# The remainders of the message tiles in a GNN edge loop: from GpSimd and VectorE to VectorE alone

## The reference, cut to what matters

```python
src, dst = edge_index
edge_feat = concatenate([x[src], x[dst], edge_attr], axis=-1)     # 512 + 512 + 64
h = mish(edge_feat @ W1 + b1)
messages = mish(h @ W2 + b2)                                      # 20000 x 512
agg = segment_sum(messages, dst, num_segments=1250)
```

## Time and profile before

| what | value |
|---|---|
| median of 3 runs | 1195.03 us (1194.22 to 1196.01) |
| the profiled execution | 1194.06 us, span of its instructions 1192.5 us |
| granted TensorE clock, mean of the span | 0.932 of full speed |
| PE busy / DVE / ACT / POOL, share of the span | 89% / 81% / 70% / 58% |

### The profile page before, as it was taken

How to read it: one execution, slowest core, us unless ns; L and a number is a source line. 1 busy time by engine, 2 the same in 40 slices (tenths; PEclk the granted TensorE clock), 3 DMA queues, 4 the chain that set the end, 5 groups by cost and what they waited for, 6 DMA issues and landing times. The chain is left out here.

```text
span 1192.5 us, 19301 instructions
## 1 busy us (share of the span) xinstructions
PE 1063.1 (89%) x5651; PEld 883.6 (74%) x5651; DVE 966.3 (81%) x1640; ACT 839.1 (70%) x1025; POOL 691.2 (58%) x541
## 2 busy tenths in 40 slices
PE   3993999999999999999999999998499995659974
PEld 2772888888888888888888888886277774559962
DVE  6651699999999999999999999999648775733366
ACT  3212899999999999999999999998235451434442
POOL 3245777777787777778778777861312210554310
PEclk9996999999999999999999999999699995779975
DMA  6736766666666666666666666660201111735545
GB/s 176 254 119 148 152 129 136 131 131 137 130 133 133 129 135 131 133 136 133 129 129 136 132 131 130 132 137 34 71 1 44 35 52 58 219 114 152 149 125 176
DMA packets 129771, 148.82 MB, mean 125 GB/s; under 512 B 73254, under 2 KB 81863, under 8 KB 129598
## 3 DMA queue, kind: packets, MB, share of 16 engines
q0 software_dynamic: 39280, 97.61, 38.3%
q1 hardware_dynamic: 90381, 50.03, 16.0%
q10 hardware_dynamic: 16, 0.02, 0.0%
HBM read 137.02 MB, written 15.69 MB: 128 GB/s over the span
## 5 line engine op out<-in xcount | busy, mean ns | idle before, releaser
L938 PE MATMUL ps<-W2h,w1l_w3l 128*128 128x512 f32 x1264 | 426.1, 398 | 0.0
L788 POOL DMA_INDIRECT gath<-dst_table,idx_sl x158 | 263.9, 1670 | 54.0 <-issue 47.1
L938 PEld LDWEIGHTS ps<-W2h,w1l_w3l 128*128 128x128 f32 x1264 | 227.4, 189 | 38.1
L938 PE MATMUL ps<-W2l,w1l_w3l 128*128 128x512 f32 x632 | 247.7, 392 | 0.0
L801 POOL DMA_INDIRECT gath<-src_table,idx_sl x156 | 188.7, 1210 | 98.5 <-issue 52.9
L810 POOL TENSOR_TENSOR msg_lo<-act,msg_hi 128x512 fp32r<-128x512 f32 x79 | 126.4, 1600 | 35.4 <-DVE msg_hi L922 35.4
L938 PEld LDWEIGHTS ps<-W2l,w1l_w3l 128*128 128x128 f32 x632 | 119.0, 188 | 26.5
L872 DVE TENSOR_TENSOR agg<-agg,ps 125x512 f32 x166 | 114.2, 688 | 15.3 <-PE ps L982 10.8
L827 ACT ACTIVATE act<-ps 128x1024 f32<-128x1024 f32 x79 | 81.2, 1027 | 37.4 <-PE ps L970 37.0
L902 DVE SCALAR_TENSOR_TENSOR act<-act,ps 128x1024 f32<-128x1024 f32 x79 | 96.0, 1215 | 2.5 <-ACT act L855 2.5
L884 DVE SCALAR_TENSOR_TENSOR act<-act,ps 128x1024 f32<-128x1024 f32 x79 | 96.0, 1215 | 2.1 <-ACT act L846 2.1
(11 more groups left out here) (321 smaller groups left out, 2380.3 us busy)
## 6 DMA issues: line engine op xcount, KB each, us to landing
f_w_raw<-in_L_ffn_w_dram SPq DMA_DIRECT2D x32, 512.0 KB, 4.6
ea_sl<-ea_scr SPq DMA_DIRECT2D x158, 64.0 KB
ea_scr<-in_edge_attr_dram POOLq DMA_DIRECT2D x1, 5000.0 KB, 19.0
w_raw<-in_L_gnn_W_dram SPq DMA_DIRECT2D x3, 1024.0 KB, 10.8
gath<-src_table,idx_sl POOLq DMA_INDIRECT x158, 3.7
gath<-dst_table,idx_sl POOLq DMA_INDIRECT x158
x_raw<-in_x_dram SPq DMA_DIRECT2D x5, 448.0 KB
src_table<-tabs SPq DMA_DIRECT2D x10, 224.0 KB
```

Source lines behind the costliest of these rows:

```text
L788: pool.indirect_dma_start(out=gath[:, k, j, :], out_offset=None, in_=dst_table[:, :], in_offset=bass.IndirectOffsetOnAxis(ap=idx_sl[:, p % ...
L938: return nc.tensor.matmul(ps_2[:, p % 2, j, :], part[:, p % 2, d, j * P:(j + 1) * P], weights[:, d, :], start=False, stop=last)
```

## The change

VectorE's subtraction L894 covers both tiles of the pair instead of the first, GpSimd's subtraction L810 is gone, and the two semaphores of the halves become one, on which ScalarE (for the free slot of `act2`) and TensorE (before L982) wait.

```diff
 # GpSimd, in step s
                 if p > 0 and exists(p):
                     add_destinations(p)
-                p = s - 4
-                if exists(p):
-                    pool.wait_ge(S["msg_hi_ready"], p + 1)
-                    need(pool, S["sum_ps"], ring_free(p))
-                    nc.gpsimd.tensor_tensor(msg_lo[:, ring(p)][:, 1], act2[:, p % A2, 1], f32(msg_hi[:, ring(p)][:, 1]), ALU.subtract).then_inc(S["msg_lo1_ready"], 1)
 # ScalarE, ahead of L833
-                        act.wait_ge(S["msg_lo0_ready"], g - A2 + 1)
-                        act.wait_ge(S["msg_lo1_ready"], g - A2 + 1)
+                        act.wait_ge(S["msg_lo_ready"], g - A2 + 1)
 # VectorE, L894
-                    nc.vector.tensor_tensor(msg_lo[:, ring(m)][:, 0], a4[:, 0], f32(msg_hi[:, ring(m)][:, 0]), ALU.subtract).then_inc(S["msg_lo0_ready"], 1)
+                    nc.vector.tensor_tensor(msg_lo[:, ring(m)], a4, f32(msg_hi[:, ring(m)]), ALU.subtract).then_inc(S["msg_lo_ready"], 1)
 # TensorE, ahead of L982
-                    pe.wait_ge(S["msg_lo0_ready"], min(m + 1, PAIRS))
-                    pe.wait_ge(S["msg_lo1_ready"], min(m + 1, PAIRS))
+                    pe.wait_ge(S["msg_lo_ready"], min(m + 1, PAIRS))
```

More of the change, by code:

```diff
@@ L733, in edge_phase @@
         names = ("eaT_ps eaT_hi eaT_lo gath_read lin1_ps exp1 inc1 sq1 ln1 quot1 h_ready h_hi h_lo lin2_ps "
-                 "exp2 inc2 sq2 ln2 quot2 msg_ready msg_hi_ready msg_lo0_ready msg_lo1_ready onehot_ready sum_ps summed w3_in w3_hi w3_lo").split()
+                 "exp2 inc2 sq2 ln2 quot2 msg_ready msg_hi_ready msg_lo_ready onehot_ready sum_ps summed w3_in w3_hi w3_lo").split()
         S = {n: sem("e_" + n) for n in names}
```

## The result

The changed kernel takes 1199.88 us (median of 9 runs, 1197.28 to 1200.70) against 1194.23 us (9 runs, 1193.30 to 1196.41) for the kernel before: ratio 1.0037, 95% interval 1.0028 to 1.0046. The two medians by themselves differ by 5.65 us or 0.47%, just above the interval, so the cost is known only as 4.4 to 5.7 us. The direction was right; the size is a quarter to a third of the forecast, and it is the size of rival 1 (1201).

What follows compares the result with a forecast made beforehand. TensorE was taken to bound the loop at 8.97 us a step, VectorE after at 9.22: 75 x 0.25 = 18.8, less 1.0, plus 0 for the end, +17.8 us, 1213 us for the median; range 1200 to 1229.

Steps and rivals of the forecast that it cites:

- rival 1: Loop: gathers and VectorE no longer collide, step 9.06 us, +5.8 us, 1201 us in all; chance 0.14.
- The bound: Loop step: TensorE sets it before at 8.97 us, VectorE after at 9.22 us, costing 0.25 us a step.
- signs named: Trace after: step near 9.22 us, VectorE not waiting for TensorE, ScalarE's wait for TensorE near nothing, stretching 0.16 us, clock 1.00.
- VectorE's own need, 8.53 us, and the 0.53 added: Loop step: VectorE's time if nobody holds it up, 8.53 us, plus 0.53 us for the larger subtraction L894.
- how the gathers and VectorE meet: Loop: stretching of VectorE instructions by GpSimd's indirect DMA, taken as 0.16 us a step, with ends 0 and 0.40.
- rival 2: Loop: gathers and VectorE collide twice in every step, step 9.46 us, +36 us, 1231 us; chance 0.13.
- The argument against rival 1: Loop: L801 will start a fixed time after TensorE's L933, in the middle of VectorE's step.
- The length of the step before: Loop before the change: 8.97 us, read from one VectorE step, L879 to L879.
- L810's direct cost: Loop: GpSimd's L810 held up the one-hot L889 twice; its going is worth 2 x 0.5 = 1 us.
- The end of the phase: Last steps of the edge phase: counted at nothing, with -1 and +2 us as ends.

Runs made afterwards that it cites:

- filler-early: Kernel before without GpSimd's subtraction from pair 7 on, plus one VectorE subtraction of 128x256 ahead of the low part: 1197.63 us, ratio 1.0024.
- 768-column: Kernel before with the subtraction shared otherwise, VectorE taking 768 of 1024 columns and GpSimd the last 256: 1193.25 us, ratio 0.9977.
- two filler kernels: Kernel before without GpSimd's subtraction, plus a 128x256 VectorE subtraction ahead of the low part (1197.63 us) or at the step's end (1204.68 us).
- the subtraction moved up: Kernel before with GpSimd's subtraction L810 placed between its source and destination gathers: 1192.45 us, ratio 0.9982.

## Why the prediction was wrong

- **The bound.** Right: TensorE before, VectorE after, in most signs named (the waits turned round, L801 held in 31 of 33 steps, 99 of 100 us busy, clock 1.00). Three signs came out otherwise: the step was 9.06 us and not 9.22, the stretching was near 0, and ScalarE's first pass still waited for TensorE in 20 steps, 3.4 us in all.
- **VectorE's own need, 8.53 us, and the 0.53 added.** Right: 9.06 forecast without collisions, 9.05 to 9.06 measured, and 9.39 with 0.33 more.
- **The failed step is the term "how the gathers and VectorE meet": "I take 0.16, the mean now".** It measured 0.00 to 0.01. The reason given, that the number of instructions of either kind stays the same, is no reason: the filler-early and the 768-column kernels have those numbers too, and show 0.17 and about 0.01. The two filler kernels do the same work, and one has the stretching and the other not, so the order of the work in the step matters. In the kernels with stretching the stretched copy started 0.6 to 1.1 us into an indirect DMA instruction, which came out at 1.0 to 1.5 (L801) or 1.6 us (L788); where the copy was not stretched, it was mostly the indirect instruction that grew, to 1.3 to 2.6 us. One of the two gives way, and the change turned it over. With 75 steps the term made 12 of the 13 us of the miss.

  The mean itself hid this. The prediction says that L922 and L908 are stretched in different steps, and holds against rival 2 that two at once would need two fitting offsets. In the trace before, both are stretched in one and the same step and neither in the next: of the 60 steps, 28 have both (9.16 to 9.21 us long but for one of 9.54) and 30 have none (28 of them 8.78 to 8.81, two 8.97). The mean of 0.16 us was 0.34 to 0.41 us in every second step and nothing in the others. In the step that ends with the stretched L922 of the earlier trace rows there stands too:

```profile
506.70 0.84 DVE L908 TENSOR_SCALAR act<-act 128x1024 f32<-128x1024 f32 x1
```

- **The argument against rival 1**, that L801 would start at a fixed time after L933. A fixed place came true, but after VectorE's one-hot instruction, and a fixed place can as well be a free one.
- **The length of the step before.** I took 8.97 us from one step; the mean over the loop was 9.00, as steps of 8.80 and 9.17 alternate and a few are longer; 8.97 itself is close to the mean of those two. That made the loop's cost 3.8 us where rival 1 has 5.8. That rival 1's 1201 came so near to the measured time is in part luck: its loop is 2.0 us too dear, and it has nothing for the end of the phase, which cost 1.1.
- **L810's direct cost**, 1 us: about right (1.6 by the run without it, 0.4 to 2.9 by its interval).
- **The end of the phase**, 0 with -1 to +2: measured +1.1, in the range but only in part by the cause named. GpSimd's four subtractions of `W3` (L814, now L809) hold up the last low part by some 1.06 us, but they did that before as well: 1.74 us against 0.68 alone then, 2.28 against 1.22 now. What differs is that the instruction itself is 0.54 us longer, and that L809, earlier against VectorE, now stretches L916 too, by 0.69 us, while the one-hot ahead of the last low part is held up by 0.23 us less. The first line is of the kernel before, the others of the changed one:

```profile
840.34 1.74 DVE L894 TENSOR_TENSOR msg_lo<-act,msg_hi 128x512 fp32r<-128x512 f32 x1
...
843.53 1.38 DVE L916 CAST msg_hi<-act 128x1024 fp32r<-128x1024 f32 x1
...
846.24 2.28 DVE L888 TENSOR_TENSOR msg_lo<-act,msg_hi 128x1024 fp32r<-128x1024 f32 x1
```

Left open: what decides which of the two gives way. The distance from the start of the indirect instruction does not decide it alone: a copy at 0.86 us is let through in the changed kernel (L893) and stretched with the subtraction moved up (L922); one at 0.55 to 0.74 is let through with 768 columns (L900), while the stretched L908, L922 and, with the filler early, L903 start at 0.58 to 0.81. The instruction ahead differs (a subtraction of two SBUF inputs ahead of L893 and L900, a one-input scalar operation ahead of L922), but L903 too follows such a subtraction and is stretched, so that is not the whole of it either. No run separates these.

## What to carry to other kernels

Where VectorE is near the bound, lengthening one of its instructions costs the excess over the slack, and the slack is read from the starts of its instructions in one undisturbed step; ask for each place of the order whether a loop through another engine runs over it, since such a loop can be full where the engine is not. A mean of collisions measured before a change is no forecast for after it, because engines of fixed order can meet at the same place in every step: in the kernels here stretched copies came in nearly every step, in every second one, or in hardly any. Keep both ends open and near to equal. And before work is moved between VectorE and GpSimd, try a smaller share or another place in GpSimd's order: here both gained 0.2%, where the whole move lost 0.4%.

## What the runs showed of the hardware that was not expected

GpSimd's indirect DMA instructions took from 0.97 to 1.97 us (gathering, L801) and from 1.53 to 2.67 us (adding, L788) in these loops, the longer ones where VectorE's copies beside them were not stretched. And one and the same filler of 0.33 us on VectorE gave 0.17 us of stretching, in the copy L903, when it stood ahead of the low part, and none when it stood at the end of the step.
